# Expert product of a routed layer: 60 whole slots and six mixed slots of four 32-row blocks in place of 71 whole slots

## What is computed

```
x = x + ln(local_attention(ln(x)))                   # 64-row windows, 16 heads
logits = t @ gate_w.T;  topk_w, topk_i = top_k(softmax(logits), 2)
for e in range(8):                                   # dense in the reference
    y = y + comb[:, e:e+1] * (silu(t @ w1[e]) * (t @ w3[e]) @ w2[e])   # 256 -> 704 -> 256
x = x + ln(y + shared_swiglu(t))                     # shared: 256 -> 384 -> 256
x = x + ln(causal_linear_attention(x));  then a gated recurrence over the rows
```

## Time and profile before

| | |
|---|---|
| median of 3 runs | 1463.41 us |
| the profiled execution's own time | 1467.51 us |
| its span in the profile | 1465.7 us |
| mean granted TensorE clock | 0.991 |
| PE busy | 1407.5 us |
| DVE busy | 871.5 us |
| ACT busy | 713.3 us |
| POOL busy | 602.1 us |

### The profile page before, as it was taken

How to read it: one execution, slowest core, us unless ns; L and a number is a source line. 1 busy time by engine, 2 the same in 40 slices (tenths; PEclk the granted TensorE clock), 3 DMA queues, 4 the chain that set the end, 5 groups by cost and what they waited for, 6 DMA issues and landing times. The chain is left out here.

```text
span 1465.7 us, 36307 instructions
## 1 busy us (share of the span) xinstructions
PE 1407.5 (96%) x13265; PEld 1223.9 (84%) x13265; DVE 871.5 (59%) x1965; ACT 713.3 (49%) x1656; POOL 602.1 (41%) x1131
## 2 busy tenths in 40 slices
PE   7999999899999999999999999998999999999996
PEld 6888887788999999999999999766777777777785
DVE  4888887474343333334433432475788888888864
ACT  4666665313444445444444442344555555555543
POOL 3666665133221222122212212545567766675533
PEclk9999999999999999999999999999999999999998
DMA  5434333352111111111111112511111112111000
GB/s 179 132 111 131 114 116 110 112 172 69 38 40 44 45 41 47 45 44 41 40 51 45 40 41 87 176 56 45 55 49 45 58 53 63 48 45 56 9 9 30
DMA packets 88733, 100.11 MB, mean 68 GB/s; under 512 B 12432, under 2 KB 75664, under 8 KB 88560
## 3 DMA queue, kind: packets, MB, share of 16 engines
q1 hardware_dynamic: 80704, 78.51, 17.4%
q0 software_dynamic: 6480, 17.70, 4.2%
q10 hardware_dynamic: 1376, 1.57, 0.3%
HBM read 63.28 MB, written 34.47 MB: 67 GB/s over the span
## 5 line engine op out<-in xcount | busy, mean ns | idle before, releaser
L1091 DVE TENSOR_TENSOR ex_gT<-ex_gT,wa_xk 128x256 f32<-128x256 f32 x71 | 29.9, 421 | 306.6 <-ACT ex_gT L1054 306.6
L956 POOL COPY slot_idx<-source 128x1 int32<-128x1 int32 x69 | 38.2, 554 | 403.1 <-PE wa_Z L1013 388.0
L986 PE MATMUL wa_P<-ex_xT,lane_w 128*128 128x128 f32 x1704 | 201.9, 275 | 0.0
L986 PEld LDWEIGHTS wa_P<-ex_xT,lane_w 128*128 128x128 f32 x1704 | 196.1, 192 | 0.2 <-issue 0.2
L1022 PE MATMUL wa_Y<-w,ex_gT 128*128 x852 | 195.7, 379 | 0.4 <-issue 0.4
L1022 PEld LDWEIGHTS wa_Y<-w,ex_gT 128*128 128x128 f32 x852 | 156.3, 190 | 19.0 <-issue 0.7
L986 PE MATMUL wa_qv<-ex_xT,lane_w 128*128 128x128 f32 x852 | 118.2, 275 | 0.0
L986 PEld LDWEIGHTS wa_qv<-ex_xT,lane_w 128*128 128x128 f32 x852 | 111.9, 192 | 3.6
L982 ACT COPY lane_w<-w 128x1408 f32 x71 | 96.9, 1365 | 7.5 <-issue 1.3
L1159 POOL TENSOR_SCALAR la_ln_ve<-la_ln_mv 128x1 f32<-128x1 f32 x128 | 33.7, 263 | 148.6 <-DVE la_ln_mv L1152 144.5
L1052 ACT ACTIVATE ex_gT<-wa_qv 128x256 f32<-128x256 f32 x71 | 27.2, 383 | 130.2 <-PE wa_qv L986 128.3
(11 more groups left out here) (289 smaller groups left out, 3297.1 us busy)
## 6 DMA issues: line engine op xcount, KB each, us to landing
yg<-ex_yo SPq DMA_DIRECT2D x71, 128.0 KB, 1.7
w<-in_w SPq DMA_DIRECT2D x16, 384.0 KB, 5.0
w<-in_w SPq DMA_DIRECT2D x16, 352.0 KB, 3.2
w<-in_w SPq DMA_DIRECT2D x16, 320.0 KB, 4.1
wa_xa<-in_x SPq DMA_DIRECT2D x32, 128.0 KB, 2.1
x<-wa_xo SPq DMA_DIRECT2D x32, 128.0 KB, 1.7
xn<-wa_xn SPq DMA_DIRECT2D x32, 128.0 KB, 1.8
xn1T<-wa_x1T SPq DMA_DIRECT2D x32, 128.0 KB, 2.1
```

What stands on the lines that cost most here:

```text
L956: e.tensor_copy(d["idx"][:], source[:, i:i + 1]).then_inc(S["idx"], 1)
L986: o = e.matmul(out, lane_w[:, i % 2, k, at:at + P], B[i % 2]["xT"][:, k, :], start=(k == 0), stop=(k == KC - 1))
```

## The change

1. **Slots.** `WHOLE` = 60 slots of 128 rows with one expert as before, and `MIXED` = 6 slots of four blocks of 32 rows, each block with an expert of its own. Experts' rows are rounded up to 32; what does not fill whole slots goes to blocks of mixed slots.
2. **A mixed slot's products** (`mixed_products`). The rows are the stationary operand, 32 columns of the array for a block, and the weights stream: for one k and one half, four products (one a block) of 352 or 416 columns, then four of 352 or 288; in all 704 columns a burst, in four bursts. Down: two bursts, each with three chunks by four blocks of 256 columns. Two transposes before and six between. The parts of mixed slot m lie in steps 8+8m to 15+8m of the whole slots' loop, between the down-product and the second half; parts 1, 2, 3, 4, 6 and 7 have a burst.
3. **Staging copies** (`fill`, on DVE). Each burst's weights are copied to `stage` first, 4 blocks by (register load, then two copies of 352, or 416 and 288, or one of 768 columns). There is one buffer, so a fill waits until PE has read the last one. It stands right behind half 0's product (g0), ahead of half 1's (g1).
4. **ACT and DVE** get the mixed slots' silu, products and copies (`mixed_copies`, `mixed_gates`).
5. **Memory.** `stage` lies where the shared weights, `wo` and `g1` are, and the mixed slots' tiles lie in `wqk` and `wvg`. These seven tensors are loaded (again) by SP at i = WHOLE - 6 (`wide`), and PE waits for them ahead of the first late unit.
6. **Routing.** `count` has 14 more short operations for the blocks' places; `places` moves from behind it to q = 4, `owners` to q = 7. The one-hot groups start at q = 6 in place of 5, with six groups a step in place of four (three and three), so that they still end at q = 8.
7. **Tables**: a `turn` every third step in place of every fourth.

The core of the diff:

```
-    SLOTS = (2 * T + E * (P - 1)) // P
+    MIXED = -(-E * (SPLIT - 1) // SPLIT)
+    WHOLE = -(-((2 * T + E * (BLOCK - 1)) // BLOCK - E * (SPLIT - 1)) // SPLIT)
+    SLOTS = WHOLE + MIXED
...
-    FIRST_HOT = 5
+    FIRST_HOT = 6
     def hot_groups(q):
-        n = (q - FIRST_HOT) * 4
-        return (range(n, n + 2), range(n + 2, n + 4)) if 0 <= n < G else ((), ())
+        n = (q - FIRST_HOT) * 6
+        return (range(n, min(n + 3, G)), range(min(n + 3, G), min(n + 6, G))) if 0 <= n < G else ((), ())
...
+            if q == 4:
                 places()
-            if q == 4:
-                owners()
+                clear_hot()
             for half in hot_groups(q + 1):
                 one_hot_groups(half)
-            if q + 1 == FIRST_HOT + G // 4 - 1:
+            if q == FIRST_HOT + 1:
+                owners()
+            if q == FIRST_HOT + 2:
                 e.wait_ge(V["mm"], G + 1)
...
+        def fill(e, s):
+            for m, n in fill_of(s):
+                if n % 2:
+                    e.wait_ge(S["mread"], 3 * m + n // 2 + 1)
+                elif m or n:
+                    e.wait_ge(S[("my", "mh0", "mh1")[n // 2]], m + (n > 0))
+                for j in range(SPLIT):
+                    at = SLOTS + SPLIT * m + j
+                    x = e.value_load(expert[0:1, at:at + 1], min_val=0, max_val=E - 1)
+                    if n < 4:
+                        k, a, b = n % 2, n // 2 * HU, HU + n // 2 * (HU + TAIL)
+                        e.tensor_copy(stage[:, j:j + 1, 0:b - a], w13[:, bass.ds(x, 1), k, a:b])
+                        c = F + TAIL + n // 2 * HU
+                        d = F + TAIL + HU if n < 2 else 2 * F
+                        o = e.tensor_copy(stage[:, j:j + 1, b - a:b - a + d - c], w13[:, bass.ds(x, 1), k, c:d])
+                    else:
+                        o = e.tensor_copy(stage[:, j, 0:KH * C].rearrange("p (k n) -> p k n", k=KH),
+                                          w2[:, bass.ds(KF * x + (n - 4) * KH, KH), :])
+                o.then_inc(S["mst"], 1)
+        def mixed_up(e, k, at, n, out):
+            for j in range(SPLIT):
+                o = e.matmul(out[block(j), 0:n], M["xT"][:, k, block(j)], stage[:, j, at:at + n],
+                             start=(k == 0), stop=(k == KC - 1))
+            return o
...
                 for half in range(2):
+                    if half:
+                        mixed_products(e, s)
...
                         o.then_inc(S[f"g{half}"], 1)
+                        if half == 0:
+                            mixed_gates(e, s)
+                            fill(e, s + 1)
...
+                if i == SLOTS - 6:
+                    e.wait_ge(S["myst"], 16 * MIXED)
+                    wide.start(e)
```

More of the change, by code:

```diff
@@ L18 @@
 LATE = 12
+BLOCK = 32
 @contextmanager
@@ L615, in owners, with clear_hot @@
         def owners():
-            then(e.tensor_tensor(cmp[:], bc(cum[:], 1, SLOTS), bc(K["slot"], 2, E), ALU.is_le))
-            then(e.tensor_reduce(se[:], cmp[:], AX_X, ALU.add))
-            then(e.tensor_scalar(expert[:], se[:], float(E - 1), None, ALU.min))
+            for ends_e, at, n in ((ends[:, 1:E + 1], 0, WHOLE), (rest_cum[:], WHOLE, MIXED * SPLIT)):
+                then(e.tensor_tensor(cmp[:, 0:n], bc(ends_e, 1, n), bc(K["slot"][:, 0:n], 2, E), ALU.is_le))
+                then(e.tensor_reduce(se[:, 0:n], cmp[:, 0:n], AX_X, ALU.add))
+                then(e.tensor_scalar(expert[:, at:at + n], se[:, 0:n], float(E - 1), None, ALU.min))
+        def clear_hot():
             then(e.tensor_copy(token[:], K["token"][:, 0:Q]))
@@ L921, with stage_views, mixed_space, experts @@
 PI_BELOW = float(np.nextafter(np.float32(np.pi), np.float32(0)))
-def experts(nc, xn1, yg, w13, lane_w, w2, slots, lead, source, expert, theta, tables, K, T, C, KC, E, SLOTS, F, later, hb, xb,
-            yb, V):
+def stage_views(stage, A, names):
+    flat, at, views = stage[:].rearrange("p j n -> p (j n)"), 0, {}
+    for name, a in names:
+        k, n = A[a].shape[0] // P, A[a].shape[1]
+        views[name] = chunks(flat[:, at:at + k * n], k)
+        at += k * n
+    assert at <= flat.shape[1]
+    return views
+def mixed_space(W, C, KC, KF, F):
+    a, b = (W[n][:].rearrange("p k n -> p (k n)") for n in ("wqk", "wvg"))
+    return {"g": a[:, 0:F], "yo": a[:, 0:C], "xT": chunks(a[:, F:F + KC * P], KC),
+            "gT": chunks(b[:, 0:KF * P], KF), "xa": b[:, KF * P:KF * P + C]}
+def experts(nc, xn1, yg, w13, lane_w, w2, slots, lead, source, expert, W, stage, tables, K, T, C, KC, E, SLOTS, MIXED, F, later,
+            wide, hb, xb, yb, mb, V):
     KF = -(-F // P)
@@ new lines, in mixed_copies @@
+        def mixed_copies(e, s):
+            for m in mixed(s, 0):
+                e.wait_ge(S["mxTp"], m + 1)
+                e.copy(M["xT"], chunks(mb[1][:, 0:C], KC)).then_inc(S["mxT"], 1)
+            for m in mixed(s, 2):
+                e.wait_ge(S["mh0"], m + 1)
+                if m >= 1:
+                    e.wait_ge(S["myst"], 16 * m)
+                e.activation(M["g"][:, 0:HU], mb[0][:, 0:HU], ACT.Silu).then_inc(S["msi0"], 1)
+            for m in mixed(s, 4):
+                e.wait_ge(S["mh1"], m + 1)
+                e.activation(M["g"][:, HU:F], mb[0][:, 0:HU], ACT.Silu).then_inc(S["msi1"], 1)
+            for m in mixed(s, 5):
+                e.wait_ge(S["mgTp"], m + 1)
+                e.copy(M["gT"][:, 0:4], chunks(mb[0], 4)).then_inc(S["mgTa"], 1)
+            for m in mixed(s, 7):
+                e.wait_ge(S["my"], m + 1)
+                e.copy(M["yo"], mb[0][:, 0:C]).then_inc(S["myo"], 1)
@@ L1430, in tensor @@
             if ahead:
+                wide.wait(e)
                 late_units(e, 0)
@@ L1967, in gpsimd @@
                         result(e, u)
-        S |= {"later": later.sem, "gates": gates.sem}
+        S |= {"later": later.sem, "wide": wide.sem, "gates": gates.sem}
         return tensor, vector, scalar, gpsimd, sync, S
```

174 lines of the change are left out of this document (137 added, 37 removed).

## The result

The changed kernel took **1449.45 us** (median of 4 runs, 1446.42 to 1451.1), the kernel before beside it 1463.44 us (median of 4, 1461.26 to 1463.89). The ratio is 0.9908, 95% interval 0.9894 to 0.9922: faster by 14.0 us. I had forecast 1447.8 us. The profiled execution took 1446.42 us, its span is 1444.6 us, its mean granted clock 0.994.

What follows compares the result with a forecast made beforehand. PE was taken to set the time, busy 540.37 of 540.79 us in the expert loop. Terms -84.9 + 56.5 + 6 + 6.8 = -15.6 us took 1463.4 to 1447.8 us (profiled execution 1451.9), range 1437 to 1461.

Steps and rivals of the forecast that it cites:

- Whole slots removed: Expert loop: 71 - 60 = 11 steps fewer at 7.72 us each, -84.9 us.
- Bursts: Mixed slots in the expert loop: four blocks take the time of one, 9.4 us a mixed slot, six of them, +56.5 us.
- 0.2 us by six bursts: Each mixed slot's bursts: going into and out of the 32-column form costs 0.2 us a burst, 1.2 us in all.
- estimate of 9.6 us for the products: Mixed slot's products by the skill's 3.07 times: 9.6 us in place of 8.5, sum 6.4 us worse, 1454 us.
- Staging copies and g1: Expert loop: fills ahead of g1 make PE idle, mainly in part 2, 1.0 us a mixed slot; +6 us, bounds 0 to 12.
- the rival of slow copies: Staging fills: 352-column copies take 0.5 us, a block 1.0 us, each fill delays g1; +31 us, 1478 us; chance 0.08.
- Routing: Shared stage, q = 6 to 8: PE idles about 8.8 to 9 us for one-hot groups, before 2.0; +6.8 us, bounds 3 to 9.
- a fall of the clock at q = 6: Routing: PE mostly idle for 4 us at q = 6, so the granted clock may fall, adding up to 1.7 us.
- Costs put at nothing: Other mixed-slot work, gathers, tables, reloaded weights and first-stage loads: covered or hidden, 0 us; reloads bound 1 us.
- All fits: Rival on staging copies and routing: copies faster, POOL keeps up, only +3 of those terms; -25.4, 1438 us; chance 0.15.
- Streams overlap by three: Rival on mixed-slot bursts: blocks overlap by three, not four; +14.8 us, 1462.6 us, no change; chance 0.07.
- not at all: Rival on mixed-slot bursts: blocks don't overlap at all, 22 us by six, 1580 us; chance 0.03.

Runs made afterwards that it cites:

- e3: The changed kernel with one full-width transpose added in the middle of each of the 24 up bursts; 1461.64 us, ratio 0.9977 to the kernel before.
- e4: The changed kernel with all four blocks' products of a mixed slot written to one 32-column strip, mixed results not computed; 1570.77 us, one run, second chip.
- e2: The changed kernel with the staging copies (fill) moved behind half 1's product (g1) instead of half 0's; 1448.74 us, ratio 0.9884 to the kernel before.
- e5: The kernel before with only the one-hot groups changed: six a step from q = 6; 1470.74 us, ratio 1.0043 to the kernel before.
- after again: The changed kernel, unaltered, run on the second chip as base for the others there; 1435.59 us, ratio 0.9901 to the kernel before.
- e9: The changed kernel with groups of four from q = 5, owners at q = 8 and fill behind half 1's product; second chip, 1426.75 us, ratio 0.9848.

## Why the prediction was right

The mechanisms came out as put: PE sets the time in the loop, DVE has room for the copies, four blocks run in the time of one, and the late start of the groups costs idle time on PE. The sum was -15.6 us and the medians' difference -14.0. Three terms were mis-sized (bursts 4.7 us too low, g1 3.0 and the routing 0.5 too high), and they nearly cancelled: that the sum came within 1.6 us of the measured difference is in part luck.

*Whole slots removed, -84.9.* A step without a part of a mixed slot still lasts 7.72 us. Right.

*Bursts, +56.5.* By the steps: four up bursts of 1.52, two down bursts of 1.63 and transposes of 0.22 + 0.66 are 10.2 us a mixed slot, six of them **+61.3**. The columns (1.19 and 1.30 a burst) and the transposes (0.88) were right. Too small was "0.2 us by six bursts" for going into and out of the 32-column form: 0.33 on each of 36 bursts, 4.7 us more in all. Of the three parts of these 0.33 us I had read the two ahead of and inside the burst from the earlier trace rows (0.09 and 0.12; now 0.09 and 0.13) and left out the third, behind it. The trace before had it too. Timeline of PE in the kernel before, the gate logits and what follows:

```profile
75.05 0.64 PE L469 MATMUL wa_P<-wa_x1T,lane_w 128*32 128x128 f32 x16
75.62 1.16 PE L484 MATMUL wa_xk<-wa_xnT,wa_wqkv 128*128 128x128 f32 x8
76.62 0.61 PE L493 MATMUL wa_qv<-wa_xnT,wa_wqkv 128*128 128x128 f32 x4
```

The eight records behind the short burst take 1.00 us, where eight cost 0.89: the same 0.11. e3 measured the whole price by itself. The rule of the Trainium skill that I weighed ("TensorE: Matmul & The Clock Gate", Part 3: 3.07 times for four packed products, there packed by rows) would have come closer in this term with the estimate of 9.6 us for the products, which last 9.34, but for another reason: e4 against the kernel after gives four times inside a burst, and what is lost is lost at the change of width. For that the Trainium skill's "TensorEngine Tiling (Array Packing)", Key Properties, has the rule that a change of tiling mode drains the engine, without a number. The 0.33 us, before, in and behind the burst, is compatible with it, but no row shows the drain itself.

*Staging copies and g1, +6 (0 to 12).* Measured 3.0 us by e2, and 2.9 by the steps (those with part 3 are 0.29 to 0.64 beyond 9.24, 2.6 in all, and 0.16 once with part 2 and once with part 4). The place was right: the fill behind part 2's burst, whose late g1 shows in the step counted as part 3, with DVE named. The 0.7 us taken for it was 0.29 to 0.64; the 0.1 for each of three other fills was in truth nothing, but for two. The pace was right (0.85 a block, 0.88 measured), and the rival of slow copies, which wanted 1.0 us a block, is out: 0.38 and 0.30 us for 416 and 288 columns, and a block comes every 0.88 us.

Together the loop's terms were -22.4, and by the sizes measured they are -84.9 + 61.3 + 3.0 = -20.6; the stretch shows -20.7.

*Routing, +6.8 (3 to 9).* Measured +6.3 in the profiled execution and +6.5 by e5. The idle time grew from 2.0 to 7.6 us, by 5.6, where I had 6.8; PE's busy time in the stretch grew by 0.7 besides (59.22 against 58.49 us), which my sum didn't have. A group that was waited for takes 0.30 us as a row where one in a stream takes 0.14, and there are five more of them. So the term came out close partly because two errors offset each other. The idle time was too high as I had worked POOL's row forward at 1.49 us a matrix and had two of the three groups behind the down-product not ready: two were ready, and each third group waited 1.07 or 1.14 us, not 1.2 to 1.8. I had also allowed for a fall of the clock at q = 6, up to 1.7 us: it came in other executions of the same kernel (after again: 2.8), not in the profiled one.

*Costs put at nothing.* Nothing shows of other work in the mixed slots (parts 6 and 7 all last the same), nor of the reloaded weights: PE is busy for 508.4 of the loop's 509.9 us, and e2 leaves 0.4 us idle. From the last slot's transposes to the attention's first late product both kernels take 12.5 us, so no wait for the reloaded weights. The stores behind the reloads in SP's queue weren't tried apart.

*The rivals.* "All fits" is out in the after kernel (1438 wanted both waits gone); e9 shows that both can go, but by other edits. "Streams overlap by three" and "not at all" are out by the burst of 1.32 us, against e4's 4.85. On the slower side nothing happened in the loop; the routing alone, without the mixed slots, gives a slower kernel (e5, ratio 1.0043).

## What to carry to other kernels

Small blocks of 32 columns with different weights can share PE at full value, as long as the blocks come round in turn and in bursts: count the burst's columns as those of one block and add 0.33 us for each burst, so make few and long ones (measured here with four blocks of fp32 at 704 to 768 columns a block and burst). Work that only fills an idle engine should stand behind, not ahead of, the operation that the bounding engine waits for, as long as it ends in time for its own reader (0.3 us were left here); cheap chains like `owners` belong where their result is wanted. These two moves and the groups of two together gave 8.8 us. With two buffers, a group of three made the bounding engine wait 1.1 us each time, most of the 1.4 us from the release of a buffer to its next tile; groups of two hid, but for the first two groups.

## What was not expected of the hardware

**The clock behind the first one-hot groups.** PE is nearly idle for some 4 us there (three groups of 0.3 us with a wait of about 1 us each). In the profiled execution of the kernel after the clock stayed at full speed, and the down-product behind took 2.67 us (316.35 to 319.02). In e2, with the same instructions in this place, it fell to the lower level. Timeline of PE in e2, then its window:

```profile
316.84 5.47 PE L407 MATMUL wa_S<-stage,lane_w 128*128 128x256 f32 x12
322.10 0.46 PE L416 MATMUL wa_Y<-sr_s_is,sr_r_is 128*128 128x66 f16 x8
```

```profile
312.00:324.00 12.00, 7.89 (x43) 5.87 (x42) 8.06 (x13) 0.59 (x1) 5.55 (x8) 0.72 0.36 113
```

The down-product took 5.26 us, twice its time: over it the granted clock is 0.50, which is 1.2 in place of 2.4 GHz, and the mean over these 12 us is 0.72. The same happened in "after again", the same kernel as the one that showed none. The trace of the kernel before has such a fall too, at another place (from 264.90 to 279.49 us, just ahead of q = 2, 0.88 on average). So one profile can't tell whether a kernel pays this: it is worth 1.7 to 2.8 us of the 4.7 us by which the runs of the kernel after differ. That this is what spreads them wasn't tried.

**A change of width on PE** costs 0.33 us a round trip around bursts (0.29 by e3), though the columns on either side stream at full pace; a third of it lies in the first full-width record behind the burst.

**Two chips** gave 1464 and 1449 us for the same kernel, a difference larger than the whole effect of this change, while the ratios agree within their intervals (0.9908 and 0.9901).
